# A two-layer feed-forward kernel with a scan between: constants multiplied in TensorE's waits, and the last layer's shared second pass begun inside its loop

## What is computed

```python
def _L0_ffn_ref(x, ...):
    logits = jnp.einsum('ed,btd->bte', gate_w, x)
    scores = jax.nn.sigmoid(logits) + gate_b
    weights, indices = jax.lax.top_k(scores, TOP_K)          # 4 of 16
    weights = weights / weights.sum(-1, keepdims=True)
    shared_out = jax.nn.silu(x @ w1_shared) * (x @ w3_shared) @ w2_shared
    h1 = jnp.einsum('btd,edc->btec', x, w1_routed)
    h2 = jnp.einsum('btd,edc->btec', x, w3_routed)
    h3 = jax.nn.silu(h1 * h2)                                # 176 wide
    experts_out = jnp.einsum('btec,ecd->bted', h3, w2_routed)
    routed_out = jnp.einsum('bted,bte->btd', experts_out, router_probs)
    return shared_out + routed_out

x = x + 0.5 * _L0_ffn_ref(_layernorm(x), ...)
x = x + _L0_attn_ref(_layernorm(x), ...)   # xp = x W_in; a = exp(-softplus(xp W_dt + b) exp(log_A)); y_t = a_t y_(t-1) + xp_t; y W_out
x = x + 0.5 * _L0_ffn_ref(_layernorm(x), ...)
```

## Time and profile before

| | |
|---|---|
| three runs | 556.86, 558.36 (median), 560.01 us |
| profiled execution | 557.04 us, of it 555.0 us from the first to the last instruction |
| mean granted clock | 0.921 |
| PE busy | 482.6 us (87%) |
| DVE, ACT, POOL busy | 430.8, 367.2, 351.4 us |
| stages | layer 0: up to about 80 us, its loop to 245; scan to 305; layer 1: to 362, its loop to 529; second pass and output to 555 |

### The profile page before, as it was taken

How to read it: one execution, slowest core, us unless ns; L and a number is a source line. 1 busy time by engine, 2 the same in 40 slices (tenths; PEclk the granted TensorE clock), 3 DMA queues, 4 the chain that set the end, 5 groups by cost and what they waited for, 6 DMA issues and landing times.

```text
span 555.0 us, 13250 instructions
## 1 busy us (share of the span) xinstructions
PE 482.6 (87%) x3206; PEld 448.7 (81%) x3207; DVE 430.8 (78%) x1464; ACT 367.2 (66%) x1109; POOL 351.4 (63%) x364
## 2 busy tenths in 40 slices
PE   2969679999999999958996961589999999999886
PEld 2957459999999999946885960379999999999765
DVE  5889757777888888884999579747777888788834
ACT  2686836777777777777874572647777777677621
POOL 3699947646777777766410507177767777777770
PEclk9988759999999999988999795579999999999989
DMA  8992125666665556654200471035555565556594
GB/s 271 393 394 102 40 84 154 191 171 176 177 209 167 171 171 161 182 162 112 69 2 0 138 239 60 3 107 163 171 163 173 169 169 161 168 171 166 175 269 139
DMA packets 61151, 88.29 MB, mean 159 GB/s; under 512 B 9499, under 2 KB 46363, under 8 KB 61107
## 3 DMA queue, kind: packets, MB, share of 16 engines
q1 hardware_dynamic: 47379, 50.29, 26.4%
q0 software_dynamic: 13728, 37.50, 26.0%
HBM read 57.22 MB, written 30.54 MB: 158 GB/s over the span
## 4 chain that ended last, share of the span: by engine, by line
PE 61%; DVE 11%; issue 10%; DMA 6%; POOL 6%; ACT 5%; SPq 1%; ACTq 0%; POOLq 0%; DVEq 0%
PE bank L1425 27%; PE bank L1477 13%; PE bank L1447 5%; DMA ys_scratch<-ring_f 2%; PE bank L1563 2%; PE bank L1488 2%; PE bank L1487 2%; PE bank L1534 2%; POOL mamba_room L627 2%; DMA lg<-ys_scratch,si 2%; PE bank L1499 1%; POOL stage L603 1%; DVE xres L1155 1%; PE bank L1645 1%; DMA raw_shared<-in_w13s 1%
## 5 line engine op out<-in xcount | busy, mean ns | idle before, releaser
L1477 PE MATMUL bank<-w_routed,ring_r 128*128 x790 | 120.5, 283 | 5.7 <-DVE ring_r L1001 5.5
L1477 PEld LDWEIGHTS bank<-w_routed,ring_r 128*128 128x128 f32 x790 | 109.9, 188 | 8.6 <-issue 8.6
L706 ACT ACTIVATE ring_r<-bank 128x256 fp32r<-128x256 f32 x158 | 60.8, 385 | 59.1 <-PE bank L1488 57.2
L1425 PE MATMUL bank<-w_routed,ring_r 128*128 x480 | 99.8, 344 | 0.0
L1425 PE MATMUL bank<-w_routed,ring_x 128*128 x468 | 94.4, 337 | 0.0
L589 POOL DMA_INDIRECT ring_f<-xn_scratch,tokidx x60 | 57.9, 964 | 45.9 <-DVE tokidx L1132 22.3
L1425 PEld LDWEIGHTS bank<-w_routed,ring_r 128*128 128x128 f32 x480 | 78.3, 195 | 0.2
L1425 PEld LDWEIGHTS bank<-w_routed,ring_x 128*128 128x128 f32 x468 | 73.8, 189 | 0.0
L589 POOL DMA_INDIRECT ring_g<-xn_scratch,tokidx x59 | 56.1, 951 | 23.0 <-issue 12.2
L558 POOL TENSOR_TENSOR w_routed<-raw_routed,w_routed 128x512 fp32r<-128x512 f32 (+1 forms) x38 | 55.3, 1490 | 20.2 <-ACT w_routed L682 20.2
L999 DVE TENSOR_TENSOR ring_r<-bank,ring_r 128x128 fp32r<-128x128 f32 x158 | 45.5, 288 | 22.4 <-ACT ring_r L706 21.4
(11 more groups left out here) (198 smaller groups left out, 1106.8 us busy)
## 6 DMA issues: line engine op xcount, KB each, us to landing
ys_scratch<-ring_f SPq DMA_DIRECT2D x152, 128.0 KB
raw_routed<-in_w13r SPq DMA_DIRECT2D x6, 704.0 KB, 12.0
xn_scratch<-w_routed SPq DMA_DIRECT2D x32, 128.0 KB, 3.9
raw_routed<-in_w2r SPq DMA_DIRECT2D x6, 512.0 KB, 13.1
raw_routed<-in_w13r SPq DMA_DIRECT2D x8, 352.0 KB, 6.0
xres<-in_x_in SPq DMA_DIRECT2D x4, 512.0 KB, 7.1
raw_routed<-in_w2r SPq DMA_DIRECT2D x8, 256.0 KB, 6.6
shared_scratch<-raw_ring SPq DMA_DIRECT2D x16, 128.0 KB, 1.7
```

Of the source, the lines that this page charges most:

```text
L706: act.activation(hT[b][0], p_hT[b][:, 0:2 * P], ACT.Copy).then_inc(s_hhi, 1)
L1425: last = pe.matmul(out, a, b, start=(q == 0), stop=(q == len(terms) - 1))
L1477: last = pe.matmul(p_y[b][:, 0:D], a, v, start=(q == 0), stop=(q == 4))
```

## The change

`stay(bank, n)` multiplies a constant matrix of ones by 512 columns of constants in half precision, n times, into a PSUM bank that nobody reads at that time. Nothing uses the result. `in_members` holds the counts of `s_dv` at the six links of `route_members`, `in_slots` those of the links of `route_slots` from the third on (15 in layer 0, 16 in layer 1). These calls are put into TensorE's program in both layers and in the scan stage. Apart from that, two of the eight pairs of layer 1's second pass go into the last four steps of the loop, and SP loads their hidden rows between the last writes of y.

```diff
+HID_FREE = 71
+IN_DRAIN = 2
...
-                with sp.Fori(1 if f else SHARED_BEHIND[-1] // UN, NS // UN) as i:
+                looped = NS // UN - (2 if f else 0)
+                with sp.Fori(1 if f else SHARED_BEHIND[-1] // UN, looped) as i:
                     for k in range(UN):
                         y_out(f, i, k)
-                if f:
-                    sp.wait_ge(s_xt, 2 * STEPS)
-                for t in range(HID_AHEAD if f else 0):
-                    hid_in(t)
+                for j in range(looped * UN, NS - YL):
+                    y_out(f, 0, j)
+                    if j == NS - YL - HID_AHEAD:
+                        sp.wait_ge(s_xt, STEPS + NT + HID_FREE)
+                    if j >= NS - YL - HID_AHEAD:
+                        hid_in(j - (NS - YL - HID_AHEAD))
...
+            def act_shared(f):
+                def stage(i, c):
+                    for pair in range(IN_DRAIN if f else 0):
+                        if isinstance(i, int) and c == NS - 2 * IN_DRAIN + pair + 1:
+                            copy_hidden(pair)
+                return stage
...
+                    in_members[f].append(chain[0])
...
+                in_slots[f] += range(begun + 3, chain[0] + 1)
...
                     b, k = c % 2, c % XG[f]
+                    if isinstance(i, int) and c < 3:
+                        stay(pb[7], 2)
...
+            def stay(bank, n):
+
+                for _ in range(n):
+                    pe.matmul(bank[:, :], hcst[:, H_ONE:H_ONE + P], hcst[:, H_I4:H_EV], start=True, stop=True)
+
+            def stay_beside(bank, counts, n):
+
+                for k in counts:
+                    pe.wait_ge(s_dv, k)
+                    stay(bank, n)
+
+            def between(n):
+
+                pe.wait_ge(s_eo, n - 1)
+                return p_yE[n % 2]
...
+            def pe_shared(f):
+
+                def stage(i, c):
+                    for pair in range(IN_DRAIN if f else 0):
+                        if isinstance(i, int) and c == NS - 2 * IN_DRAIN + pair:
+                            turn_hidden(pair)
+                        if isinstance(i, int) and c == NS - IN_DRAIN + pair:
+                            shared_out(pair)
+                return stage
...
                     if s < NT:
                         turn_x(f, s)
+                    if f == 1 and s < 2:
+                        stay(pb[3], 2)
...
                 for n in range(SH_BEFORE if f == 0 else 0):
                     shared_step(n)
+                if f == 0:
+                    pe.wait_ge(s_hcst, 16)
+                stay(pb[6], 10)
+                for n, k in enumerate(in_members[f]):
+                    stay_beside(pb[6], (k,), 4 if n < 3 else 2)
                 count(f)
                 for n in range(SH_BEFORE, SH_ENDS if f == 0 else SH_BEFORE):
                     shared_step(n)
+                stay_beside(between(SH_ENDS - 1) if f == 0 else pb[6], in_slots[f], 2)
                 tile_experts(f)
                 for t in range(NT):
                     pick(f, t)
+                    stay(between(steps_in_picks(t).start - 1) if f == 0 else pb[6], 1)
                     for n in steps_in_picks(t) if f == 0 else ():
                         shared_step(n)
...
+                stay(pb[7], 10)
                 pe.wait_ge(s_m, base + NT)
...
-                                  (LAG_E, pe_experts(f)), (LAG_T, pe_ht(f, base))], XG[f])
+                                  (LAG_E, pe_experts(f)), (LAG_T, pe_ht(f, base)), (LAG_Y, pe_shared(f))], XG[f])
                 if f == 1:
-                    turn_hidden(0)
-                    for pair in range(1, NT // 2):
+                    turn_hidden(IN_DRAIN)
+                    for pair in range(IN_DRAIN + 1, NT // 2):
                         turn_hidden(pair)
                         shared_out(pair - 1)
                     shared_out(NT // 2 - 1)
                 if f == 0:
+                    stay(pb[2], 6)
                     pe.wait_ge(s_wm, 16)
...
                     def turn(c):
+                        if c < 2:
+                            stay(pb[2], 2)
...
                     def outputs(c):
+                        if c >= NMC - MT:
+                            stay(pb[3], 4)
...
                     staggered([(1, inputs), (4, outputs), (0, turn), (1, step_sizes)])
+                    stay(pb[3], 8)
```

More of the change, by code:

```diff
@@ L417, in staggered @@
                         stage_of(s - lag)
+        chain = [0]
+        in_members, in_slots = [[], []], [[], []]
         block = ctx.enter_context(nc.Block())
@@ L863, in _ @@
                 pipeline(act, NS, [(LAG_H + 1, act_first(f, base)), (LAG_T + 1, act_ht(f)), (LAG_X, act_x(base)),
-                                   (LAG_H + 1, act_silu(base)), (LAG_Y + 1, act_slot_out(f)), (LAG_Y + 1, act_roots(f))],
+                                   (LAG_H + 1, act_silu(base)), (LAG_Y + 1, act_slot_out(f)), (LAG_Y + 1, act_roots(f)),
+                                   (LAG_Y + 1, act_shared(f))],
                          looped=ADDED_FROM)
-                for pair in range(NT // 2 if f else 0):
+                for pair in range(IN_DRAIN if f else NT // 2, NT // 2):
                     copy_hidden(pair)
@@ L954, in _ @@
         def _(dve):
-            chain = [0]
             def link(ins):
@@ L1067, in route_slots @@
             def route_slots(f):
+                begun = chain[0]
                 ones = cst[:, C_ONE:C_ONE + 1].broadcast_to((P, NT * NE))
```

## The result

The changed kernel takes 556.22 us (median of 12 runs, 551.06 to 559.66), the kernel before 558.61 (12 runs, 554.32 to 562.02). The ratio is 0.9943, 95% interval 0.9916 to 0.9970: about 3 us faster, at the edge of what can be told from no change, where 7.5 were forecast. The median is inside the forecast range. The two profiled executions don't even differ: 557.48 us against 557.04, span 555.5 against 555.0. Yet TensorE's mean granted clock went from 0.921 to 0.988. In that execution the clock did nearly what the change wants, and the time didn't follow. The ratios leave out one run of the changed kernel (559.66 us) and one of e7 (775.64 us, mean clock 0.616), which were slow for their kernel; the medians have them in.

What follows compares the result with a forecast made beforehand. Bound: TensorE's low clock after waits, and DVE in the routing. Scan start -2.4, layer 1 start -2.0, its loop -2.2, end -1.7, counts +0.3, layer 0 +0.6: -7.4, 557.04 to 549.6; median 1.3 above, 550.9 us (546.5 to 558).

Steps and rivals of the forecast that it cites:

- Layer 0's block: 30 constants ahead of layer 0's first pick: 6.9 us long, `tokidx` 2.6 us late, 0.6 us late in sum.
- Of the 2.6 us some comes back in the loop's first steps: Layer 0's loop start: faster first steps return between 1.0 and 2.6 us of the late `tokidx`; 2.0 taken.
- The end: Last shared pass with two pairs moved into layer 1's loop: fourth pair's transposes begin 1.7 us earlier, bounds 0 to 3.5.
- from there to the end nothing changes: From the fourth pair's transposes on: time to the end stays the same, so their earlier start, 1.7 us, is the gain.
- a low clock behind the wait for the loads: Ahead of the fourth pair: named only for the end's lower bound, a gain of 0, with loads landing in 4.2 us.
- Rival 1: Clock still falls in some gaps; one or two of three starts lost, 2 to 4.4 us, about 554.5; chance 0.22.
- Layer 1's loop start: First tiles of layer 1's loop at the high clock: 2.2 us early, bounds 0 to 2.4.
- if gathered rows are there: Condition on the 2.2 us gain at layer 1's loop start: the tiles' gathered rows must have landed.
- The scan start: Scan stage's transposes and first products at the high clock: 2.4 us early, bounds 0 to 2.6.
- Layer 1's start: First tiles of layer 1's first pass at the high clock: 2.0 us early, bounds 0 to 2.3.
- One constant: Cost of one 512-column constant on TensorE: 0.23 us at the high clock, bounds 0.21 to 0.235; 0.45 at the low.
- The counts: Routing counts behind 28 constants: halved at the high clock; layer 1's end 0.3 us late, layer 0's 0.5 given back.

Runs made afterwards that it cites:

- e7: Changed kernel without layer 0's block of 30 constants, last shared pass and its loads in old order, ten constants ahead of that pass: 551.77 us, ratio 0.9884.
- e1: Changed kernel without the block of 30 constants ahead of layer 0's first pick: 551.44 us, ratio 0.9879 to the kernel before.
- e2: Changed kernel with 15 constants instead of 30 ahead of layer 0's first pick: ratio 0.9884 to the kernel before.
- e10: Changed kernel with 60 constants instead of 30 ahead of layer 0's first pick: ratio 1.0032 to the kernel before.
- e3: Changed kernel with ten more constants in the wait ahead of the fourth pair's transposes in the last shared pass: 554.07 us, ratio 0.9933.
- e4: Changed kernel with layer 1's shared second pass back behind the loop and SyncE's old order, all constants kept: median 556.04 us, ratio 0.9962.
- e6: Changed kernel without layer 0's block of 30, and with ten constants in the wait ahead of the fourth pair's transposes: 550.21 us, ratio 0.9866.
- e12: e11 with the fourth pair's two loads ahead of the last writes of y instead of the fill at the end: 549.90 us, ratio 0.9828.
- e5: Kernel before with only the last shared pass's move into the loop and SyncE's new order, no constants anywhere: ratio 0.9981.
- e9: e8 without the fill at the end, with the fourth pair's two loads ahead of the last writes of y: 546.69 us, ratio 0.9817.
- e8: e6 also without layer 0's 28 constants ahead of the counts, single ones behind picks and ten ahead of gathers: 549.07 us, ratio 0.9838.
- e11: e8 also without the constants at layer 1's counts, chain and picks, leaving those ahead of starts and in the tail: 550.28 us, ratio 0.9866.

## Why the prediction was wrong

**Layer 0's block: the step that failed first.** The 30 ran back to back for 6.6 us, and `tokidx` came at 78.81, 2.7 us late where 2.6 were forecast (3.4 against e1). That agreement is luck. I had the first pick at 63.8 and DVE's last 13 picks at 13.0 us "at the high clock"; it came at 61.51, and they took 15.3 us (61.87 to 77.21), with the clock at 0.50 from 67.2 to 74.0 and waits of up to 1.75 us for PE. So the picks made up 1.1 us of the block (the same 13 took 16.4 us before), not 3.4. What failed outright is "Of the 2.6 us some comes back in the loop's first steps... I take 2.0". The loop start gave 0.4 us (13.67 to 13.26), because of its tiles only the first had run at the low clock throughout, and e1, e2 and e10 show that nothing later makes up for a late first gather. The term was +0.6; e1 measures it at 3.4 us at the first gather and 3.7 at the loop's end, and the medians differ by 4.8.

**Loop 0** had no term and took +1.9 us. The loops of 155.3 us and more go with one stall. ACT in the changed kernel:

```profile
233.06 0.38 ACT L732 ACTIVATE ring_f<-bank 128x256 f32<-128x256 f32 x1 [2.06 <-DMA ys_scratch<-ring_f]
```

ScalarE waits 2.06 us to evict an output, for the write of y before it, while GpSimd gathers rows of y for the sums already. It isn't lateness as such: e10 is later still and has none. Seven profiles have such a wait of 1.4 to 2.3 us between 229 and 242 us (changed, e1, e2, e3, e4, e6, e12), and their loop 0 is 155.3 to 156.4 us long; in the other seven the longest there is 1.3 (e5), and theirs is 153.8 to 154.6. Whether it is how writes and gathers fall together wasn't tried, and the cause stays open.

**The end: the second that failed.** Counted from the loop's first output products, so without what came before, the last tile's output was 2.4 us late (2.0 taken) and the fourth pair 1.7 us early (163.4 against 165.1 us), just as forecast. What failed is "from there to the end nothing changes". I had taken the wait in front of these transposes for a landing time and nothing else. Behind it the clock was at 0.50, and from the fourth pair to the last products it took 12.3 us instead of 9.1: 3.2 us given back. e3, which fills the wait, and e9, which removes it, show it from both sides. I had priced "a low clock behind the wait for the loads" in a bound only. The trace of before had the warning: the 0.8 in slice 39 of the earlier trace rows, which I read over, is the first pair's products at the low clock, behind a wait for loads. Rival 1, a clock that falls in a gap, so came true at a place for which it had no number (and, in five of the experiments' profiles, for 3.4 us at the start of the scan stage, at a price of 0.6 to 0.8 us).

**Layer 1's loop start: mis-sized.** Forecast -2.2, measured -0.6. Four profiles (e3, e8, e9, e10) have 12.0 to 12.1 us there, which is -1.7 to -1.8, the mechanism at nearly full size. In seven of the other eight one of the first gathers lands late. The changed kernel and then e3, transposes of the third gathered tile, whose gathers were issued at 361.18 and 362.52 us:

```profile
365.32 0.44 PE L1468 MATMUL bank<-cst,ring_f 128*128 128x128 f32 x2 [1.62 <-DMA ring_f<-xn_scratch,tokidx]
```

```profile
365.27 0.44 PE L1468 MATMUL bank<-cst,ring_f 128*128 128x128 f32 x2 [0.28 <-DMA ring_f<-xn_scratch,tokidx]
```

That is 4.1 us against 2.75. Why a gather is late no run here shows. My clause "if gathered rows are there" was the condition, and the full gain came in four of the twelve profiles that have these constants.

**What was right.** The scan start (forecast -2.4, measured -2.2, and 58.7 us in seven kernels). Layer 1's start (-2.0, measured -2.0 by e11). One constant: 0.2157 us from start to start (28 from 34.17 to 40.21), inside the bounds and below the 0.23 taken; the Trainium skill's figure (TensorE: Matmul & The Clock Gate, "Wait — 56ns, not 53.3ns?") agrees to the digit. The counts: halved (the second kind from 1.91 to 1.03 us); in layer 1 they ended 28.3 us behind the layer's start against 28.5 without constants ahead of them (e11), 0.2 us gained where 0.3 lost were forecast, since the constants are shorter.

With the measured terms in place of mine the sum is -2.2 (scan) -2.0 (layer 1's start) -0.6 (loop start) +1.4 (end and loop 1: +2.4 - 1.0) -0.3 (layer 1's routing) +2.3 (g0 and its start) +1.9 (loop 0) = +0.5 us, that of the profiled executions. The 12 runs of each put it at -2.4; the 3 us between are within the spread of single executions.

## What to carry to other kernels

Filling a wait on TensorE is only free while the engine that waits for TensorE has other work or buffers left: count the buffers between the two, and make the filling no longer than that lead, here about 3 of 6.6 us. Look where the clock falls after the edit, not only where it fell before: work that is pulled forward until it waits for a load opens a gap of its own, and taking the wait away by an earlier load (tail 6.0 us below the kernel before) beats filling it (4.3). Constants paid here where a dense stage follows a wait; in the routing, whose path another engine sets, they gave 0.3 us or nothing. And compare the clock of every run, not only that of the profiled one.

## What the runs showed that I had not expected

- One wait of 2.24 us after some microseconds of dense work was followed by a clock of 0.50, and the pass ran slow from 535.21 (transposes of 1.05 us) to 542.70 (0.60 again). A wait as long (2.23 us) in e5 was followed by 3.4 us at 0.50, from 537.9, and the eight constants ahead of the scan stage didn't prevent such a stretch in five of twelve profiles: in e1 they themselves took 2.54 us instead of 1.90.
- Of the first six gathers of layer 1 one takes 3.8 to 4.3 us to its tile's transposes instead of 2.7 to 2.9 in the others: the third in the changed kernel, the fourth in e4 and e2, the sixth in e1, e6, e7 and e11, none in e3, e8, e9 and e10.
- A loop of 79 steps varies by 2.6 us in layer 0 and, among the eleven with the moved tail, by 2.5 in layer 1. A ledger by stage sees edits of 0.3 us in the stretches that repeat; the time of a single run doesn't see 3. Much of that spread goes with the clock: 0.999 and 551.06 us, 0.981 and 559.66 in the changed kernel, 1.000 and 555.98, 0.984 and 563.27 in e10. Which of the two leads the other these figures don't say.
